# Sandwich-norm attention and ternary expert layer on one core: the turned queries are copied from PSUM by ScalarE, and two norms in a row take one power instead of two

## The reference, cut to what matters

```python
# H=16 query heads, 4 key/value heads, head width 8
def rmsnorm(x, w):
    return x * jax.lax.rsqrt(jnp.mean(x * x, axis=-1, keepdims=True) + 1e-06) * w
def attn(hidden, ...):
    x = hidden
    x = x + global_latent_attn(rmsnorm(x, norm1_w), ...)   # causal over all tokens
    x = x + local_gqa_attn(rmsnorm(x, norm2_w), ...)       # a window of 32 tokens
    return x
def ffn(x, ...):
    h = layernorm(x, eps=1e-05) * ln_gamma + ln_beta
    ...                                  # router, top expert, ternary weights
x = x + _layernorm(attn(_layernorm(x), ...))
x = x + _layernorm(ffn(_layernorm(x), ...))
```

## Time and profile before

| what | value |
|---|---|
| median of 3 runs | 725.56 us (723.76 to 728.81) |
| the profiled execution, its own time | 719.88 us |
| its span, first to last instruction | 718.1 us |
| mean granted clock of TensorE in it | 0.95 |

### The profile page before, as it was taken

One profiled execution on the slowest core, in us unless ns is written; L12 is line 12 of the kernel. 1 busy time (PEld: TensorE's weight loads), 2 busy tenths in 40 slices (PEclk: granted clock), 3 DMA queues, 4 the chain that ended last, 5 costly groups with the idle time before them and its releaser, 6 DMA issues.

```text
span 718.1 us, 16201 instructions
## 1 busy us (share of the span) xinstructions
PE 563.5 (78%) x5986; PEld 286.4 (40%) x6001; DVE 399.8 (56%) x1014; ACT 353.6 (49%) x482; POOL 248.8 (35%) x688
## 2 busy tenths in 40 slices
PE   1228559877887999989888989889997999767574
PEld 1115225424444443534344453344434433533452
DVE  2672866455465675667646557553645552654355
ACT  1022224863662578456836756677685588103000
POOL 3524685376257146513370311501123030050100
PEclk9999869997999999999999999999999999987797
DMA  8000000000000000000000000000000000000000
GB/s 229 1 0 1 1 2 2 1 1 2 1 3 1 2 9 2 2 1 9 1 3 1 9 1 2 8 2 2 5 5 1 2 9 2 1 0 8 1 1 9
DMA packets 8812, 6.21 MB, mean 9 GB/s; under 512 B 1944, under 2 KB 8096, under 8 KB 8736
## 3 DMA queue, kind: packets, MB, share of 16 engines
q10 hardware_dynamic: 3424, 2.64, 1.3%
q1 hardware_dynamic: 5312, 2.52, 1.3%
HBM read 4.11 MB, written 1.05 MB: 7 GB/s over the span
## 4 chain that ended last, share of the span: by engine, by line
PE 48%; DVE 22%; POOL 15%; issue 9%; ACT 4%; SPq 0%; DVEq 0%; DMA 0%; POOLq 0%; ACTq 0%
PE osum_g L922 12%; PE scores L896 9%; PE misc L1032 5%; PE misc L1043 4%; PE scores L890 3%; ACT prob L756 3%; PE misc L922 3%; PE misc L940 3%; DVE early L1354 2%; DVE qT L1248 1%; PE misc L872 1%; PE misc L971 1%; DVE early L1392 1%; PE misc L863 1%; POOL rs_g L625 1%
## 5 line engine op out<-in xcount | busy, mean ns | idle before, releaser
L756 ACT ACTIVATE prob<-scores 128x1024 f32<-128x1024 f32 (+3 forms) x352 | 307.6, 933 | 206.4 <-PE scores L896 203.6
L922 PE MATMUL osum_g<-prob,V 128*32 128x256 f32 (+1 forms) x2304 | 174.3, 391 | 14.8 <-ACT oTs_g L765 6.0
L896 PE MATMUL scores<-qT,kT 64*128 64x512 bf16 (+3 forms) x760 | 128.2, 357 | 29.0 <-ACT prob L756 15.7
L896 PEld LDWEIGHTS scores<-qT,kT 64*128 64x128 bf16 x760 | 35.1, 93 | 139.0 <-issue 124.9
L922 PEld LDWEIGHTS osum_g<-prob,V 128*32 128x32 f32 x2304 | 52.1, 110 | 77.8 <-issue 56.6
L693 POOL TENSOR_SCALAR_AFFINE_SELECT prob<-prob 128x512 f32<-128x512 f32 x64 | 40.9, 658 | 119.2 <-ACT prob L756 118.9
L713 POOL TENSOR_SCALAR frs<-fmv 128x1 f32<-128x1 f32 x16 | 3.4, 210 | 157.5 <-DVE fmv L1408 157.3
L940 PE MATMUL misc<-identb 128*128 128x256 bf16 x248 | 38.2, 312 | 20.0 <-DVE kT L1237 7.6
L1043 PE MATMUL misc<-t2T,h1p 128*128 128x512 bf16 x177 | 43.8, 397 | 10.6 <-DVE h1p L1385 8.6
L1032 PE MATMUL misc<-early,t1T 128*128 128x256 bf16 x384 | 44.1, 273 | 0.7 <-DVEq L1374 0.7
L1032 PEld LDWEIGHTS misc<-early,t1T 128*128 128x128 bf16 x384 | 36.8, 98 | 7.4 <-issue 3.1
(11 more groups left out here) (218 smaller groups left out, 803.3 us busy)
## 6 DMA issues: line engine op xcount, KB each, us to landing
X<-in_L_attn_hidden_dram SPq DMA_DIRECT2D x8, 128.0 KB, 4.5
early<-in_L_ffn_expert_w_dram ACTq DMA_DIRECT2D x1, 1024.0 KB, 7.7
out_dram<-X SPq DMA_DIRECT2D x16, 64.0 KB, 1.5
rope<-in_rope_dram SPq DMA_DIRECT2D x1, 256.0 KB, 3.7
early<-in_L_ffn_shared_w_dram ACTq DMA_DIRECT2D x2, 128.0 KB, 8.2
wraw_l<-in_L_attn_l_wq_dram ACTq DMA_DIRECT2D x1, 64.0 KB, 2.6
ident<-in_ident_dram SPq DMA_DIRECT2D x1, 64.0 KB, 2.5
wraw_g<-in_L_attn_g_wq_dram SPq DMA_DIRECT2D x1, 64.0 KB
```

The source lines that it names most:

```text
L756: act.activation(prob[:, n % NP, :, lo:hi], src, ACT.Exp, scale=float(HD) ** -0.5).then_inc(exp_done, 1)
L896: ins = pe.matmul(o[:, :, c:c + w], kT[a][rows, g, P * (t % kept[a]):P * (t % kept[a]) + P], qT[a][rows, b % Q_KEPT[a], 2 * g:2 * g + 2, q ...
L922: ins = pe.matmul(o[32 * m:32 * m + 32, q:q + w], V[a][:, t % kept[a], g, :], prob[:, n % NP, j, c:c + w], start=(first and k == 0), stop= ...
```

## The change

Three things change in the code. POOL's factors for the G front and for `fxa` are computed with fewer instructions. `q_copy` moves from DVE to ACT, with its waits. And four numbers of the planner change: `qT` is now 0.95 us of ACT, `onT` and `fz` have other durations, and PE's idle time from which fillers go in is 1.341 instead of 1.439.

```diff
@@ COST, KNOBS
-... "qT": [(PE, 0.55), (DVE, 0.7)],
-    "oT": [(PE, 0.588), (DVE, 0.758)], "onT": [(PE, 0.304), (ACT_E, 0.26)],
+... "qT": [(PE, 0.55), (ACT_E, 0.95)],
+    "oT": [(PE, 0.588), (DVE, 0.758)], "onT": [(PE, 0.282), (ACT_E, 0.325)],
-... "fz": [(DVE, 0.833)],
+... "fz": [(DVE, 0.672)],
-    "idle": 1.439,
+    "idle": 1.341,
@@ POOL, stat of G
-                    rsqrt(r[:, 0, :], v, EPS_LN)
-                    link(pool.tensor_tensor(r[:, 1, :], r[:, 0, :], r[:, 0, :], ALU.mult))
-                    link(pool.tensor_tensor(r[:, 1, :], r[:, 1, :], v, ALU.mult))
-                    rsqrt(r[:, 2, :], r[:, 1, :], EPS_RMS)
-                    pool.tensor_tensor(r[:, 3, :], r[:, 0, :], r[:, 2, :], ALU.mult).then_inc(rs_ready[a], 1)
+                    pool.tensor_scalar(r[:, 0, :], v, 1.0, EPS_LN, ALU.mult, ALU.add)
+                    link(pool.tensor_scalar(r[:, 2, :], v, 1.0 + EPS_RMS, EPS_RMS * EPS_LN, ALU.mult, ALU.add))
+                    pool.tensor_tensor(r[:, 1, :], r[:, 0, :], mhalf[:, 0:2], ALU.pow)
+                    pool.tensor_tensor(r[:, 3, :], r[:, 2, :], mhalf[:, 0:2], ALU.pow).then_inc(rs_ready[a], 1)
@@ POOL, fxa
-                rsqrt(r[:, 2, :], fmv[:, 1, :, 1], EPS_LN)
-                link(pool.tensor_tensor(r[:, 3, :], r[:, 2, :], r[:, 2, :], ALU.mult))
-                link(pool.tensor_tensor(r[:, 3, :], r[:, 3, :], fmv[:, 1, :, 1], ALU.mult))
-                rsqrt(r[:, 4, :], r[:, 3, :], EPS_LN)
-                pool.tensor_tensor(r[:, 5, :], r[:, 2, :], r[:, 4, :], ALU.mult).then_inc(frs_ready, 1)
+                link(pool.tensor_scalar(r[:, 4, :], fmv[:, 1, :, 1], 1.0 + EPS_LN, EPS_LN * EPS_LN, ALU.mult, ALU.add))
+                pool.tensor_tensor(r[:, 5, :], r[:, 4, :], mhalf[:, 0:2], ALU.pow).then_inc(frs_ready, 1)
@@ ACT (the same function is taken out of DVE's code, with dve for act and tensor_copy for copy)
+            def q_copy(a, b, i):
+                s = ("qT", a, b, i)
+                wait_full(act, s)
+                old = b - Q_KEPT[a]
+                if old >= 0:
+                    act.wait_ge(qk_done, UNIT[(a, old, *units_of(a, old)[-1])] + 1)
+                act.copy(qT[a][:, b % Q_KEPT[a], :, P * i:P * i + P],
+                                bank(s)[:].bitcast(BF16).rearrange("p (m q) -> p m q", m=H // 2)).then_inc(free(s), 1)
+                act.wait_ge(free(s), TAKE[(*s, 0)][1] + 1)
+                act.sem_inc(qT_ready[a], 1)
```

More of the change, by code:

```diff
@@ L108 @@
     "xT": [(PE, 0.394), (ACT_E, 0.525)], "proj": [(PE, 0.8), (DVE, 2.8), (POOL, 0.5)], "newton": [(POOL, 1.9)],
-    "split": [(DVE, 2.209)], "expand": [(POOL, 2.134)], "kT": [(PE, 0.8), (DVE, 0.6)], "qT": [(PE, 0.55), (DVE, 0.7)],
-    "oT": [(PE, 0.588), (DVE, 0.758)], "onT": [(PE, 0.304), (ACT_E, 0.26)], "wo": [(PE, 0.314), (DVE, 0.411)],
+    "split": [(DVE, 2.209)], "expand": [(POOL, 2.134)], "kT": [(PE, 0.8), (DVE, 0.6)], "qT": [(PE, 0.55), (ACT_E, 0.95)],
+    "oT": [(PE, 0.588), (DVE, 0.758)], "onT": [(PE, 0.282), (ACT_E, 0.325)], "wo": [(PE, 0.314), (DVE, 0.411)],
     "oevac": [(ACT_E, 0.3)], "pv": [(PE, 0.388)], "fstat": [(DVE, 1.169), (POOL, 0.662)],
@@ L122 @@
 KNOBS = {
-    "idle": 1.439, "share": 0.406, "most": 24, "fronts": 2, "feed": 33.972, "warm": 0.15, "from": 40.0,
+    "idle": 1.341, "share": 0.406, "most": 24, "fronts": 2, "feed": 33.972, "warm": 0.15, "from": 40.0,
 }
@@ L790, in fact @@
                 act.activation(ez, z, ACT.Tanh, scale=0.5).then_inc(ez_ready, 1)
-            run = {"weights": weights, "xT": xT_copy, "qk": exp, "oevac": o_copy, "onT": onT_copy, "fhT": fhT, "frouter": frouter,
+            run = {"weights": weights, "xT": xT_copy, "qT": q_copy, "qk": exp, "oevac": o_copy, "onT": onT_copy, "fhT": fhT, "frouter": frouter,
                    "fw1s": fw1s, "fact": fact}
@@ L1176, in norm @@
                     if a == G:
[L1177 removed]
+                        dve.tensor_scalar(Hn[:, b % 3, i, :], src[:, i, :], mv[a][:, i, 0:1], rs[a][:, 1, i:i + 1],
                                           ALU.subtract, ALU.mult)
@@ L1415, in _ @@
             run = {"weights": weights, "prep": prep, "ternary": ternary, "wturn": wturn, "scales": scales,
-                   "stat": stat, "norm": norm, "proj": proj, "split": split, "kT": k_copy, "qT": q_copy,
+                   "stat": stat, "norm": norm, "proj": proj, "split": split, "kT": k_copy,
                    "oT": o_scale, "wo": residual, "fstat": fstat, "fxa": fxa, "fh": fh_norm,
```

13 lines of the change are left out of this document (1 added, 12 removed).

## The result

The changed kernel takes 752.29 us (median of 4 runs, 751.33 to 753.31) against 724.68 us for the kernel before beside it (723.76 to 728.81): a ratio of 1.0376 [1.0326, 1.0426]. It is 3.8% slower. I had forecast 717.6 us and a range of 704 to 731. The profiled execution took 751.33 us, its span is 749.6 us.

What follows compares the result with a forecast made beforehand. PE sets the pace from 200 to 600 us, chains of single steps set it at both ends; -2.5 - 1.2 - 1.3 + 0 - 3.0 = -8.0 us from 725.6 gives 717.6 us, range 704 to 731.

Steps and rivals of the forecast that it cites:

- The roots: POOL's factors: a G `stat` 1.0 us shorter, `fxa` 1.9 us shorter, 8 of each, 23.2 us of chain.
- The copy on ACT: Each query copy takes 1.03 us and holds ACT for about 1.2 us, 32 of them some 38 us.
- the bound from below, 0.60: Lower estimate of ACT's query copy in us, from the 128x512 float32 copy if bf16 pairs went at twice the rate.
- The start: First fronts: first scores at 45.1 instead of 48.73 us; -2.5 us carried, and -1.2 more for other early gains.
- my second rival: Early gains are absorbed before 200 us, leaving -4 us or less, 722 us; chance 0.20.
- The end: Last local front 1.1 us and last block's `fxa` 1.9 us faster, together -3.0 us.
- The middle: Between start and end: -1.3 us from DVE's waits in `fxa`, and 0 for the balance of DVE relieved and ACT burdened.
- The fillers at 0: 330 fillers for 252 stand in expected PE waits, so counted as 0, at most 10 us.
- [N]othing for a better clock either: Middle: no gain counted from TensorE's granted clock, already at 0.99 and 1.00.
- My first rival: ACT becomes the bound, 16 query copies delaying what follows by 6 to 19 us; 733 us with 15; chance 0.15.
- PE's busy time from 400 to 600 below 178 us: Middle of the kernel: one of the signs set down to show the forecast wrong.

Runs made afterwards that it cites:

- e1: Kernel before with only POOL's shorter factors (new roots), old order and copies: 717.87 us, ratio 0.9897.
- e2: Kernel before with only the query copies moved to ACT, old order and roots: 727.45 us, ratio 1.0041.
- e3: Changed kernel with the planner's old numbers, so new roots and copies in the old order: 718.32 us, ratio 0.9904 to the kernel before.
- e4: Kernel before with the planner's four new numbers, so new order with old roots and copies on DVE: 760.48 us, ratio 1.0509.
- e5: Changed kernel with 184 of its 330 filler matmuls left out, other steps in the same order: 750.92 us, ratio 1.0354 to the kernel before.
- e10: Changed kernel with other planner bonuses, drawn at random for the lowest closing clock: 693.95 us, ratio 0.9572 to the kernel before.

## Why the prediction was wrong

The forecast was -8.0 us and the kernel is 27.6 slower. By its own steps:

- The roots: right. 1.86 us was worked out for a G `stat`, the rows have 1.89; for `fxa` 1.9 us less, and the way to `fh` is 1.87 shorter. e1 shows what they are worth by themselves, 1.0%, with an interval from 0.6 to 1.5; the terms for them in the sum (2.0, 1.3 and 1.9 us) make 0.7%.
- The copy on ACT: right in size (1.03 forecast, 1.015 measured; 1.18 between two starts, 1.2 forecast), and the bound from below, 0.60, was far off. That exponents queue behind it costs nothing net that e2 could show.
- The start: first scores at 45.1, forecast and measured. But of the 2.5 us that I carried nothing was left at block 1's G output (143.71 against 143.49). There my second rival, that early gains are absorbed, was right. In the old order e3 has the first scores at 45.2 and block 1 at 145.39, 1.9 us later than before.
- The end: -3.0 us, forecast and measured, in the same two pieces, 1.1 and 1.9. The first of them has some luck in it: the working, scores 1.8 us earlier of which 0.9 is taken back, gives 0.9 and not the 1.1 that was put down.
- **The middle is the step that failed.** The prediction says there: "For the balance I take 0, with bounds of -8 us [...] and +19". Both bounds came from loads, DVE relieved and ACT burdened by 19 us. That the new plan moves steps between 150 and 450 us I treated as cost free: I had walked three places of it, the start, the third front and the end, and let them stand for a program whose order differs in hundreds of lines. e4 puts +5.1% on just this term, which has no entry in my sum. Without it the number would stand: e3 measured 718.32 us, for 717.6, and 1.0% below the kernel before, for 1.1%. That agreement is partly luck, since e3 runs the old order, for which the terms of the start and the end were not worked out: by its residual rows it is 0.8 us ahead of before at 201 us (forecast 3.7), 4.2 behind at block 7, and gains 4.8 at the end (forecast 3.0).
- The fillers at 0 were right in effect (e5), though for another reason than the one given: they do not all fall into gaps that are there anyway, the rest buys back clock.
- "[N]othing for a better clock either: it is at 0.99 and 1.00 there" was a reading of the old order. That the clock could fall there, and in the changed kernel did, to 0.94 and 0.97, I did not ask.

My first rival named the right sign, with a bound of +19 for the middle. As the cause of this loss its mechanism falls: e4 is slow with no query copy on ACT, e2 with all of them is within 1% of before, and e10 runs with the same ACT load in 694 us. As a price inside the old order it may exist, in the 2 to 9 us that e3 and e2 lose between blocks 1 and 7. The sign "PE's busy time from 400 to 600 below 178 us", which I had set down for the forecast being wrong, did not appear (181.3); the loss was in the 200 us before. A rival that says "the new order as a whole is worse" was missing, and with it a range that goes to 752. What spoke for it was to be had before any run: the planner's closing clock rises from 800.1 to 842.7. By the factor of 0.66 found since that is +28 us, less 8 for the code, some 745 us. That is a reckoning after the fact, but its sign needed no factor.

## What to carry to other kernels

Where a planner or scheduler orders a kernel by a table of costs, a change of the table is a new draw of the whole order, and may outweigh by far the code change that it comes with: measure the code in the frozen order and the new order with the old code, and only then the two together. The ten weights stayed while the costs changed, and other weights gave the best version here, so choose them anew, by the planner's own length first (with a scatter of 14 us at 0.66 for one, an estimate from the table, it ranks orders that lie more than some 20 us apart there) and on the chip for the last candidates. And a prediction for such a change needs a term for the order, read from the whole plan and not from the places at which one happens to look.

## What the runs showed of the hardware

- In the changed kernel each PE wait of 4 us or more in the middle of full work was followed by half clock (4.83 us before 159.26, 4.84 before 241.39, 4.40 before 317.98), the second although 18 filler matmuls ran directly ahead of it. In such a stretch 16 turns take 1.06 us instead of 0.64.
- Taking 184 fillers out of the changed kernel lowered the mean granted clock of its span from 0.93 to 0.902 and left the time where it was (750.9 against 752.3).
- One and the same program differs in granted clock from run to run, and mostly in time with it: of the 25 runs of the kernel before that stood beside e1 to e4, the five at 719.6 to 720.2 us have clocks of 0.945 to 0.947, and those at 729.07 and 729.13 have 0.918; one at 725.05 has 0.944, so the mean clock doesn't say all. The profiled execution of before was one of the lower kind (719.9 us, 0.95), which is why the sum had to be carried to the median by 5.7 us.
- ACT copies 128x1024 bf16 from PSUM to SBUF in 1.015 us, DVE in 0.691. Two powers of 128x2 in a row without a link between them start 0.65 us apart on POOL and take 0.69 each (15.01 and 15.66 us in the changed kernel).
